# Recurrent scan of a decoder: products on single 32x32 diagonal blocks in place of block-diagonal 128x128 matrices

## The chip, the core and the metric

The kernel runs on one core of a Trainium2 chip. The metric is the device time of one execution in microseconds, as the median of several executions. The core has TensorE (matrix products, results in PSUM), VectorE (DVE), ScalarE (ACT), GpSimd (POOL) and the DMA queues, which SyncE (SP) issues. Each engine runs its own instructions in order and waits for the others on semaphores.

## The reference, cut to what matters

The whole program is a decoder of two layers (RWKV-7 time mixing, cross attention, a mixture of experts, four Mamba layers, feature attention, a quantised feed-forward part). The change touches only the recurrence of the RWKV-7 part, for 4 sequences of 512 tokens with 4 heads of 64 channels:

```python
def step(S, inp):
    rt, dt, kt, vt, at, bt = inp
    sa = jnp.einsum('bhij,bhj->bhi', S, at)
    S = S * dt[:, :, None, :] + sa[..., None] * bt[:, :, None, :] + vt[..., None] * kt[:, :, None, :]
    y = jnp.einsum('bhij,bhj->bhi', S, rt)
    return (S, y)
_, ys = jax.lax.scan(step, S0, (r_, decay, k_, v_, a_, b_))
```

## The kernel before, in words

`rwkv_scan` (from L658) does this recurrence in chunks of 32 tokens. One turn of its loop treats a tile of 128 tokens, that is 4 chunks (NCH) for each of 4 heads (H1), and there are 16 turns (NT); the first and the last are written out, the others are a hardware loop on every engine. A turn consists of these steps, in TensorE's order:

1. `tr` (L955): six 128x128 transposes bring the decayed keys of the tile to token rows; ACT copies them to `tm`.
2. `levels` (L945): for each head, 32 small products (64 rows by 32 columns of weights) give four 32x32 matrices per chunk: BA, BR, KA, KR. DVE picks the causal entries level by level into `Ac` (L875). Between heads, `state_step` (L928) carries the state of the previous tile through one chunk, and DVE adds it up (L854). `state_y` (L936) multiplies the states by `RT`; ACT copies the outputs (L769).
3. POOL spreads the four compact matrices of each head to block-diagonal 128x128 matrices `Abd` (L750): it multiplies a broadcast copy by a mask of blocks.
4. `q` (L970, L971): for each head a transpose of BA, and KA times the values. ACT copies both into `PQX` (L781, L782).
5. The doubling, called the k steps below (L981 to L983): (1 - A)^-1 times the right-hand side X = [W | U] by five steps X += P X, with P and its transpose Q squared each time. Steps run k = 0 to 4, and heads h = 0 to 3 within each. A head's step has a product for Q (L981), one for P (L982), both left out at k = 4, and one for X (L983), all 128x128x128 on block-diagonal matrices. ACT copies P and Q out of PSUM (L786), DVE adds X (L883). After k = 0 DVE's queue has `decay(it + 1)` for the next turn (L816 to L821), and after k = 1 ACT's queue has `factors(it + 1)` (L762, L763).
6. `rp` (L987): W times BR; DVE adds it into `RT` (L888) and then makes the factors of the next turn (L832 to L846).
7. `mn` (L995 to L997): 48 products of 32 rows by 64 columns give the transfer matrices of the chunks. DVE writes `MT` (L897) and ACT `NN` (L791); the next turn's `tr` waits for both.
8. `y1`: two products with zeros clear two banks (L1003), then BR times U and KR times the values are added (L1005, L1006). POOL copies the next values to `vs` after it (L744).

A wait is written in two ways. `wait_ge` alone leaves the wait to the instruction that follows. `hold` (L71 to L75) waits with an instruction of its own, which also adds 1 to a semaphore `passed`; in the trace it is an EVENT_SEMAPHORE of line L75, with an ALU_OP or FUSED_REGOPS of L74 for the value waited for. Each fp32 product of TensorE stands as two records of LDWEIGHTS and MATMUL in the trace, so 12 products are 24 records.

Of the kernel before, what the change touches and what calls it, by code (L numbers as in the profile page):

```python
# [165 lines left out]
def shape_constants():  # L166
# [3 lines left out]
    for w in (32, 16, 8):  # L170
# [13 lines left out]
        "block_mask": np.repeat((np.arange(P)[:, None] // 32 == np.arange(4)[None]).astype(np.float32)[:, :, None], 32, 2),  # L184
# [473 lines left out]
def rwkv_scan(nc, g, m):  # L658
# [15 lines left out]
    with ExitStack() as ctx:  # L674
# [11 lines left out]
        Abd = [sb(f"rs_Abd{h}", [P, 4, P]) for h in range(H1)]  # L686
        PQX = [sb(f"rs_PQX{h}", [P, 3 * P]) for h in range(H1)]
# [4 lines left out]
        blockmask = sb("rs_blockmask", [P, NCH, CH])  # L692
# [6 lines left out]
        BA, BR, KA, KR = range(4)  # L699
# [9 lines left out]
        pool = signal("pool", "vs " + each("xa") + each("bd"))  # L709
# [21 lines left out]
        with nc.Block() as block:  # L731
            @block.sync
            def _(sp):
                for dst, src in ((levelmask, g["level_masks"]), (blockmask, g["block_mask"]), (reset, g["chunk_reset"]),
                                 (eye64, g["eye_twice"]), (bound, g["carry_bound"])):
                    sp.dma_start(full(dst), src).then_inc(masks_in, 16)

            @block.gpsimd
            def _(po):
                begin(po, pool)  # L740
                po.wait_ge(masks_in, 80)
                with po.Fori(0, NT) as it:
# [3 lines left out]
                    for h in heads:  # L746
                        nc.gpsimd.tensor_copy(PQX[h][:, 2 * P:2 * P + N1], tm[:, AT, h * N1:(h + 1) * N1]).then_inc(*pool(f"xa{h}"))  # L747
                    for h in heads:
                        po.wait_ge(*dve.at(f"ac{h}{LAST}", it))
                        nc.gpsimd.tensor_tensor(  # L750
                            Abd[h][:, :, :].rearrange("p m (q t) -> p m q t", q=NCH),
                            Ac[h][:, :, :, :].rearrange("p x y (o t) -> p (x y) o t", o=1).broadcast_to([P, 4, NCH, CH]),
                            blockmask[:, :, :].rearrange("p (o q) t -> p o q t", o=1).broadcast_to([P, 4, NCH, CH]),
                            ALU.mult).then_inc(*pool(f"bd{h}"))

            @block.scalar
            def _(a):
# [14 lines left out]
                def body(it, state=True, following=True):  # L772
# [6 lines left out]
                    for h in heads:  # L779
                        a.wait_ge(*pe.at(f"q{h}", it))  # L780
                        nc.scalar.activation(PQX[h][:, P:2 * P], bank[h][:, P:2 * P], ACT.Copy)  # L781
                        nc.scalar.activation(PQX[h][:, 2 * P + N1:], bank[4 + h][:, N1:P], ACT.Copy).then_inc(*act(f"q{h}"))  # L782
                    for k in range(4):
                        for h in heads:
                            a.wait_ge(*pe.at(f"n{h}{k}", it))
# [2260 lines left out]
```

## Time and profile before

| | us |
|---|---|
| median of 3 runs | 3923.72 (3921.09 to 3923.76) |
| the profiled execution | 3921.58 |
| its span in the trace | 3919.7 |
| busy: TensorE, DVE, ACT, POOL | 3082.4, 2929.5, 1879.3, 1883.7 |
| the scan's part of the span | about 228 to 847 |

The profile's page gives busy times and costly groups of instructions by line. Answers of the trace then show one stretch of time, one engine or one line. In a timeline, a row is one or several like instructions in a row: start, time from the first start to the last end, engine, line, operation, output and inputs, shape, count, and in brackets the idle time before with what ended it. PEclk is the share of full TensorE clock that was granted: 0.50 is the lower of its two levels (1.2 GHz), 1.00 the higher (2.4 GHz).

### The profile page before, as it was taken

What the parts mean: (1) busy time and instruction counts of PE and PEld (TensorE: products, weight loads), DVE (VectorE), ACT (ScalarE), POOL (GpSimd) and SP (SyncE); (2) the same over time, 40 slices, a digit from 0 to 9 for tenths busy, and PEclk for the clock granted to TensorE, in tenths of its full rate; (3) what the DMA queues carried; (4) which work ended last, traced back from release to release, by engine and by line L of the source; (5) the groups of instructions that cost most, each with busy time, mean ns of one, the idle gap of its engine ahead of it and who ended that gap; (6) DMA issues with size and microseconds to landing.
All of it is one profiled execution on the core that took longest, in us unless ns stands there. A gap on an engine that the chain in (4) does not pass through costs nothing. (4 is left out here: it accounts for less than half of the span.)

```text
span 3919.7 us, 46678 instructions
## 1 busy us (share of the span) xinstructions
PE 3082.4 (79%) x16262; PEld 1734.7 (44%) x16262; DVE 2929.5 (75%) x3862; ACT 1879.3 (48%) x2899; POOL 1883.7 (48%) x961
## 2 busy tenths in 40 slices
PE   8968888865638965898889988899888998666823
PEld 3457777753325742333434334343343443333512
DVE  4656666665711123999999999999999999996588
ACT  2433333222411114766677666677666775523434
POOL 0011111121221021779888888888888888861100
PEclk9967777777858986999999999999999999997966
DMA  1000000000032323344443444434444444331000
GB/s 42 0 7 1 0 0 0 0 6 19 0 109 87 117 79 102 129 149 140 162 140 133 148 141 161 143 130 158 141 152 143 135 153 140 129 118 35 1 20 22
DMA packets 120614, 342.23 MB, mean 87 GB/s; under 512 B 14763, under 2 KB 45698, under 8 KB 119714
## 3 DMA queue, kind: packets, MB, share of 16 engines
q1 hardware_dynamic: 114594, 332.01, 25.0%
q0 software_dynamic: 3072, 6.00, 0.8%
q10 hardware_dynamic: 2816, 2.62, 0.2%
q8 instruction: 64, 1.05, 0.1%
q14 instruction: 68, 0.56, 0.0%
HBM read 328.31 MB, written 14.68 MB: 88 GB/s over the span
## 5 line engine op out<-in xcount | busy, mean ns | idle before, releaser
L1950 POOL TENSOR_TENSOR mb_h<-mb_h,mb_BC 128x1024 f32<-128x1024 f32 x512 | 1212.8, 2389 | 406.8 <-DVE mb_h L2197 406.8
L2197 DVE TENSOR_TENSOR_SCAN mb_h<-mb_dA,mb_bx 128x1024 f32<-128x1024 f32 x512 | 1170.5, 2286 | 23.8 <-ACT mb_dA L2064 6.0
L2300 PE MATMUL mb_y<-mb_h,ident 128*128 128x512 f32 x2048 | 1000.0, 628 | 215.2 <-POOL mb_h L1950 213.4
L2064 ACT ACTIVATE mb_dA<-mb_delta,mb_A 128x511 f32<-128x511 f32 x1024 | 664.7, 713 | 415.3 <-DVE mb_h L2197 409.4
L2300 PEld LDWEIGHTS mb_y<-mb_h,ident 128*128 128x128 f32 x2048 | 387.7, 198 | 790.2 <-issue 415.3
L2193 DVE TENSOR_TENSOR mb_bx<-mb_du,mb_BC 128x1024 f32<-128x1024 f32 x512 | 630.3, 1231 | 42.7 <-DMA mb_BC<-mamba_BC 6.7
L744 POOL COPY rs_vs<-rw_v 128x256 f32 x16 | 9.8, 612 | 571.2 <-PE rs_p L1006 338.9
L245 PE MATMUL mb_p<-mb_xT,mb_in_w 128*128 128x512 f32 x512 | 238.1, 609 | 23.3 <-ACT mb_sz L1990 16.7
L245 PE MATMUL mb_p<-mb_upad,mb_convd 128*128 128x512 f32 x512 | 225.0, 592 | 0.8 <-ACT mb_upad L1978 0.8
L1674 DVE TENSOR_TENSOR me_h<-me_s,me_p 128x320 f32<-128x320 f32 x64 | 31.2, 488 | 242.6 <-ACT me_s L1651 242.6
L883 DVE TENSOR_TENSOR rs_PQX<-rs_p,rs_PQX 128x128 f32<-128x128 f32 x320 | 85.8, 290 | 114.8 <-PE rs_p L983 113.7
L245 PEld LDWEIGHTS mb_p<-mb_xT,mb_in_w 128*128 128x128 f32 x512 | 99.1, 196 | 153.5 <-issue 118.9
L1628 POOL DMA_INDIRECT me_y<-expert_results,slot x32 | 30.8, 963 | 256.2 <-DMA expert_results<-me_oe 246.8
L245 PEld LDWEIGHTS mb_p<-mb_upad,mb_convd 128*128 128x128 f32 x512 | 96.8, 189 | 124.1 <-issue 124.1
L245 PE MATMUL me_p<-me_xeT,me_W 128*128 128x320 f32 x512 | 141.4, 437 | 0.9 <-ACT me_xeT L1639 0.9
L786 ACT ACTIVATE rs_PQX<-rs_p 128x256 f32<-128x256 f32 x256 | 93.1, 383 | 71.6 <-PE rs_p L983 71.6
L245 PE MATMUL mb_p<-mb_out_w,mb_yg 128*128 128x256 f32 x512 | 121.0, 379 | 0.0
L2064 ACT ACT_TABLE_LOAD x91 | 116.8, 1283 | 1.6
L245 PEld LDWEIGHTS me_p<-me_xeT,me_W 128*128 128x128 f32 x512 | 97.5, 192 | 43.7 <-issue 4.8
L750 POOL TENSOR_TENSOR rs_Abd<-rs_Ac,rs_blockmask 128x512 f32<-128x512 f32 x64 | 81.0, 1266 | 65.8 <-DVE rs_Ac L875 65.5
L2389 POOL TENSOR_TENSOR fa_A<-fa_E,fa_sm 128x512 f32<-128x512 f32 x32 | 35.8, 1122 | 149.0 <-DVE fa_sm L2516 144.3
L875 DVE COPY_PREDICATED rs_Ac<-rs_levelmask,rs_p 128x64 f32<-128x64 uint32 (+1 forms) x256 | 62.8, 246 | 54.1 <-POOL rs_PQX L747 17.0
(439 smaller groups left out, 5554.2 us busy)
## 6 DMA issues: line engine op xcount, KB each, us to landing
mb_BC<-mamba_BC SPq DMA_DIRECT2D x256, 1024.0 KB, 5.2
me_W<-in_L_ffn_W SPq DMA_DIRECT2D x24, 1024.0 KB, 9.2
mb_in_w<-in_L_attn_in_proj_w SPq DMA_DIRECT2D x4, 1024.0 KB, 8.2
mb_convd<-in_mamba_taps SPq DMA_DIRECT2D x4, 1024.0 KB, 10.2
expert_rows<-me_zero SPq DMA_DIRECT2D x1, 2560.0 KB, 10.1
x<-in_x SPq DMA_DIRECT2D x4, 512.0 KB, 5.3
me_xe<-expert_rows SPq DMA_DIRECT2D x8, 256.0 KB, 10.7
expert_results<-me_oe ACTq DMA_DIRECT2D x8, 256.0 KB, 7.6
```

The source lines that it names most:

```text
L245: i = nc.tensor.matmul(out, lhsT, rhs, start=k == 0, stop=k == len(pairs) - 1)
L750: nc.gpsimd.tensor_tensor(Abd[h][:, :, :].rearrange("p m (q t) -> p m q t", q=NCH), Ac[h][:, :, :, :].rearrange("p x y (o t) -> p (x y) o ...
L786: nc.scalar.activation(PQX[h][:, 0:2 * P], bank[h][:, 0:2 * P], ACT.Copy).then_inc(*act(f"n{h}{k}"))
L875: nc.vector.copy_predicated(later(Ac[h][:, :, :, :].rearrange("p x y t -> p (x y) t"), l), later(levelmask[:, l, :].rearrange("p (k t) -> ...
L883: nc.vector.tensor_tensor(X, bank[4 + h][:, 0:P], X, ALU.add).then_inc(*dve(f"x{h}{k}"))
L1674: nc.vector.tensor_tensor(h[:, k, :], s1[:, k % 2, :], bank[3 + 2 * (k % 2)][:, 0:CAP], ALU.mult).then_inc(*dve(f"h{k}"))
L1950: tt(hk, hk, buffer(k, it)[:, 1, :, :], ALU.mult).then_inc(*pos(f"hc{k}{part}"))
L2064: i = av(dA[k % 2][:, c, s, 1:], delta[:, it % 2, mc, 1:], ACT.Exp, scale=A[:, MC * layer(it) + mc, n:n + 1])
L2193: tt(full(bx), du[c][:, :].rearrange("p (o t) -> p o t", o=1).broadcast_to([P, SU, T]), buffer(k, it)[:, 0, :, :], ALU.mult).then_inc(*dvs ...
L2197: nc.vector.tensor_tensor_scan(flat(h[k % NBUF][:, c, :, :]), flat(dA[k % 2][:, c, :, :]), flat(full(bx)), 0.0, ALU.mult, ALU.add).then_in ...
L2300: i = mm(ybank[c][:, :], m.ident[:, :], h[k % NBUF][:, c, s, :], start=False, stop=e == HALF - 1 and s == SU - 1)
L2389: nc.gpsimd.tensor_tensor(A[:, u % NE, :, :], E[:, u % NE, :, :], sm[:, u % NE, :].rearrange("p (h o) -> p h o", o=1).broadcast_to([P, HC, ...
```

## The change

The block-diagonal matrices `Abd` are gone, and with them POOL's spreading, the mask `block_mask` and its load. Every product on such a matrix becomes four products ("quads"), each on one chunk's 32x32 block, at the same partitions 32q to 32q + 31 for its weights, its moving operand and its output. P and Q shrink to 32 columns (`PQ`), so ACT copies 64 elements per partition in place of 256; X stays 128 wide. The step k = 3 leaves out Q, which k = 4 doesn't use. The transpose of BA becomes a product with the identity block. The four quads of one product write into one PSUM bank at different partitions, except in `rp`, where each goes to a bank of its own (4 to 7); DVE's addition of `RT` becomes four. TensorE's waits in `q` and in the k steps become `hold`s. DVE has one `hold` per head less, since it needn't wait for POOL before it writes `Ac`.

```diff
         Ac = [sb(f"rs_Ac{h}", [P, 2, 2, CH]) for h in range(H1)]
-        Abd = [sb(f"rs_Abd{h}", [P, 4, P]) for h in range(H1)]
-        PQX = [sb(f"rs_PQX{h}", [P, 3 * P]) for h in range(H1)]
+        PQ = [sb(f"rs_PQ{h}", [P, 2, CH]) for h in range(H1)]
+        X = [sb(f"rs_X{h}", [P, 2, N1]) for h in range(H1)]
...
-                    for h in heads:
-                        po.wait_ge(*dve.at(f"ac{h}{LAST}", it))
-                        nc.gpsimd.tensor_tensor(
-                            Abd[h][:, :, :].rearrange("p m (q t) -> p m q t", q=NCH),
...
-                            ALU.mult).then_inc(*pool(f"bd{h}"))
...
-                        nc.scalar.activation(PQX[h][:, P:2 * P], bank[h][:, P:2 * P], ACT.Copy)
-                        nc.scalar.activation(PQX[h][:, 2 * P + N1:], bank[4 + h][:, N1:P], ACT.Copy).then_inc(*act(f"q{h}"))
+                        nc.scalar.activation(PQ[h][:, 1, :], bank[h][:, CH:2 * CH], ACT.Copy)
+                        nc.scalar.activation(X[h][:, 1, :], bank[4 + h][:, N1:P], ACT.Copy).then_inc(*act(f"q{h}"))
...
                             if l == 0:
                                 hold(v, m, pe.at(f"lv{h}", it))
-                                hold(v, m, pool.at(f"bd{h}", it - 1))
...
-                    nc.vector.tensor_tensor(RT[:, :, :], bank[4][:, 0:W2].rearrange("p (c n) -> p c n", c=DC), rt_of(it), ALU.add).then_inc(*dve("rp"))
+                    for q in range(NCH):
+                        s = slice(CH * q, CH * q + CH)
+                        i = nc.vector.tensor_tensor(RT[:, :, s], bank[4 + q][:, 0:DC * CH].rearrange("p (c n) -> p c n", c=DC), rt_of(it)[:, :, s], ALU.add)
+                    i.then_inc(*dve("rp"))
...
                     for h in heads:
-                        t.wait_ge(*pool.at(f"bd{h}", it))
-                        nc.tensor.transpose(bank[h][:, P:2 * P], Abd[h][:, BA, :], m.ident[:, :])
-                        mm(bank[4 + h][:, N1:P], Abd[h][:, KA, :], vs[:, h * N1:(h + 1) * N1], start=True, stop=True).then_inc(*pe(f"q{h}"))
+                        hold(t, m, dve.at(f"ac{h}{LAST}", it))
+                        for s in quads:
+                            mm(bank[h][s, CH:2 * CH], chunks(h, BA)[s, :], m.ident[s, s], start=True, stop=True)
+                        for s in quads:
+                            i = mm(bank[4 + h][s, N1:P], chunks(h, KA)[s, :], vs[s, h * N1:(h + 1) * N1], start=True, stop=True)
+                        i.then_inc(*pe(f"q{h}"))
                     for k in range(5):
                         for h in heads:
                             if k == 0:
-                                t.wait_ge(*act.at(f"q{h}", it))
+                                hold(t, m, act.at(f"q{h}", it))
+                                if h == 0:
+                                    hold(t, m, pool.at(f"xa{H1 - 1}", it))
                             else:
-                                t.wait_ge(*act.at(f"n{h}{k - 1}", it))
-                                t.wait_ge(*dve.at(f"x{h}{k - 1}", it))
-                            Pk = PQX[h][:, 0:P] if k else Abd[h][:, BA, :]
+                                hold(t, m, act.at(f"n{h}{k - 1}", it))
+                                hold(t, m, dve.at(f"x{h}{k - 1}", it))
+                            Pk, Qk = (PQ[h][:, 0, :] if k else chunks(h, BA)), PQ[h][:, 1, :]
+                            if k < 3:
+                                for s in quads:
+                                    mm(bank[h][s, CH:2 * CH], Pk[s, :], Qk[s, :], start=True, stop=True)
                             if k < 4:
-                                mm(bank[h][:, P:2 * P], Pk, PQX[h][:, P:2 * P], start=True, stop=True)
-                                mm(bank[h][:, 0:P], PQX[h][:, P:2 * P], Pk, start=True, stop=True)
-                            mm(bank[4 + h][:, 0:P], Pk, PQX[h][:, 2 * P:3 * P], start=True, stop=True).then_inc(*pe(f"n{h}{k}"))
+                                for s in quads:
+                                    mm(bank[h][s, 0:CH], Qk[s, :], Pk[s, :], start=True, stop=True)
+                            for s in quads:
+                                i = mm(bank[4 + h][s, 0:P], Pk[s, :], X[h][s, :, :].rearrange("p x i -> p (x i)"), start=True, stop=True)
+                            i.then_inc(*pe(f"n{h}{k}"))
...
-                        i = mm(bank[4][po:po + N1, hp * P:(hp + 1) * P], W[h], Abd[h][:, BR, :], start=True, stop=True)
+                        for q, s in enumerate(quads):
+                            i = mm(bank[4 + q][po:po + N1, hp * CH:hp * CH + CH], W[h][s, :], chunks(h, BR)[s, :], start=True, stop=True)
...
-                        mm(y_out(h), Abd[h][:, BR, :], U[h], start=False, stop=False)
-                        i = mm(y_out(h), Abd[h][:, KR, :], vs[:, h * N1:(h + 1) * N1], start=False, stop=False)
+                        for s in quads:
+                            mm(y_out(h)[s, :], chunks(h, BR)[s, :], U[h][s, :], start=False, stop=False)
+                        for s in quads:
+                            i = mm(y_out(h)[s, :], chunks(h, KR)[s, :], vs[s, h * N1:(h + 1) * N1], start=False, stop=False)
```

## Rows read from the trace of the kernel before

**Rows 1.** The page's head.
```profile
span 3919.7 us, 46678 instructions
```

**Rows 2.** Windows: stretch, length, busy us (instructions) per engine, granted clock; one turn.
```profile
548.20:556.70 8.50, 7.67 (x318) 6.36 (x316) 5.18 (x21) 0.75 (x3) 4.04 (x7) 0.50 0.00 0
556.70:560.40 3.70, 2.79 (x15) 2.80 (x16) 2.05 (x4) 1.91 (x10) 1.79 (x2) 0.50 0.00 0
560.40:571.20 10.80, 10.03 (x83) 9.78 (x83) 6.22 (x20) 7.23 (x16) 0.00 (x0) 0.95 0.00 0
...
574.90:577.80 2.90, 2.90 (x96) 2.85 (x95) 2.77 (x4) 0.00 (x0) 0.00 (x0) 1.00 0.00 0
577.80:581.80 4.00, 3.89 (x22) 3.68 (x20) 4.00 (x10) 0.00 (x0) 0.00 (x0) 0.60 0.00 0
```

**Rows 3.** Timeline of DVE in the same turn.
```profile
550.12 1.43 DVE L875 COPY_PREDICATED rs_Ac<-rs_levelmask,rs_p 128x64 f32<-128x64 uint32 x4 [0.97 <-POOL rs_PQX L747]
...
563.89 0.69 DVE L816 TENSOR_TENSOR_SCAN rs_dif<-rs_reset,rw_w 128x256 f32<-128x256 f32 x1
...
566.64 0.88 DVE L883 TENSOR_TENSOR rs_PQX<-rs_p,rs_PQX 128x128 f32<-128x128 f32 x4
...
575.03 0.42 DVE L888 TENSOR_TENSOR rs_RT<-rs_p,rs_rt 128x256 f32<-128x256 f32 x1 [0.93 <-PE rs_p L987]
...
581.32 1.62 DVE L897 SCALAR_TENSOR_TENSOR rs_MT<-rs_eye,rs_Eend,rs_p 128x64 f32<-128x64 f32 x8
```

**Rows 4.** Timeline of ACT in the same turn.
```profile
556.64 0.45 ACT L769 ACTIVATE rw_w<-rs_p 128x128 f32 x2 [7.75 <-PE rs_p L936]
...
566.75 1.49 ACT L762 ACTIVATE rs_Ep<-rs_dif 128x1536 f32<-128x1536 f32 x1
...
569.30 1.19 ACT L786 ACTIVATE rs_PQX<-rs_p 128x256 f32<-128x256 f32 x4
```

**Rows 5.** Timeline of TensorE's matrix products in the same turn.
```profile
552.81 1.29 PE L945 MATMUL rs_p<-rs_left,rs_right 64*32 64x32 f32 x64
...
555.51 0.36 PE L936 MATMUL rs_p<-rs_S,rs_RT 64*32 64x64 f32 x4
555.59 0.33 PE L945 MATMUL rs_p<-rs_left,rs_right 64*32 64x64 f32 x4
...
557.61 0.47 PE L970 MATMUL rs_p<-ident,rs_Abd 128*128 128x128 f32 x1 [1.11 <-POOL rs_Abd L750]
...
558.19 0.42 PE L970 MATMUL rs_p<-ident,rs_Abd 128*128 128x128 f32 x1
...
562.24 0.39 PE L982 MATMUL rs_p<-rs_Abd,rs_PQX 128*128 128x128 f32 x2
...
566.97 0.49 PE L981 MATMUL rs_p<-rs_PQX 128*128 128x128 f32 x2 [0.77 <-DVE rs_PQX L883]
...
574.15 0.66 PE L987 MATMUL rs_p<-rs_Abd,rs_PQX 128*64 128x128 f32 x8 [0.39 <-DVE rs_PQX L883]
...
577.82 0.71 PE L1003 MATMUL rs_p<-ident,rs_zeros 128*128 128x128 f32 x4
...
583.90 1.52 PE L955 MATMUL rs_p<-ident,rs_base 128*128 128x128 f32 x6 [2.20 <-ACT rs_NN L791]
```

**Rows 6.** Lines L945 (552.79 to 553.49) and L74 (553.4 to 553.6): counts, first and last start.
```profile
L945 PE MATMUL rs_p<-rs_left,rs_right x52: 237/238/291, 552.8 to 553.5; 64*32 64x32 f32 x48, 64*32 64x64 f32 x4
...
L74 PEldq ALU_OP  x1: 32/32/32, 553.5 to 553.5; - x1
```

**Rows 7.** Line L75, the holds: TensorE's 557.0 to 557.45, DVE's 549.7 to 550.1.
```profile
L75 PEldq EVENT_SEMAPHORE  x2: 51/51/51, 557.1 to 557.4; - x2
...
L75 DVEq EVENT_SEMAPHORE  x2: 21/21/21, 549.8 to 550.0; - x2
```

**Rows 8.** Timelines of DVE in the last turn and of SyncE before the scan.
```profile
839.54 1.62 DVE L897 SCALAR_TENSOR_TENSOR rs_MT<-rs_eye,rs_Eend,rs_p 128x64 f32<-128x64 f32 x8 [2.65 <-PE rs_p L997]
...
228.53 0.43 SPq L736 DMA_DIRECT2D rs_blockmask<-in_block_mask  x1
```

More of the change, by code:

```diff
@@ L698, in rwkv_scan @@
         AT, BT, KT = range(3)
-        BA, BR, KA, KR = range(4)
+        BA, BR, KA, KR = ((x, y) for x in range(2) for y in range(2))
         heads = range(H1)
@@ L708, in rwkv_scan @@
         act = signal("scalar", "tm " + each("q") + " ".join(f"n{h}{k}" for k in range(4) for h in heads) + " nn")
-        pool = signal("pool", "vs " + each("xa") + each("bd"))
+        pool = signal("pool", "vs " + each("xa"))
         dvf, acf = signal("vector_f", "cum dif left right base end"), signal("scalar_f", "ep em")
@@ L733, in _ @@
             def _(sp):
-                for dst, src in ((levelmask, g["level_masks"]), (blockmask, g["block_mask"]), (reset, g["chunk_reset"]),
+                for dst, src in ((levelmask, g["level_masks"]), (reset, g["chunk_reset"]),
                                  (eye64, g["eye_twice"]), (bound, g["carry_bound"])):
@@ L740, in _ @@
                 begin(po, pool)
-                po.wait_ge(masks_in, 80)
+                po.wait_ge(masks_in, 64)
                 with po.Fori(0, NT) as it:
@@ L780, in body @@
                         a.wait_ge(*pe.at(f"q{h}", it))
-                        nc.scalar.activation(PQX[h][:, P:2 * P], bank[h][:, P:2 * P], ACT.Copy)
-                        nc.scalar.activation(PQX[h][:, 2 * P + N1:], bank[4 + h][:, N1:P], ACT.Copy).then_inc(*act(f"q{h}"))
+                        nc.scalar.activation(PQ[h][:, 1, :], bank[h][:, CH:2 * CH], ACT.Copy)
+                        nc.scalar.activation(X[h][:, 1, :], bank[4 + h][:, N1:P], ACT.Copy).then_inc(*act(f"q{h}"))
                     for k in range(4):
                         for h in heads:
+                            n = 2 if k < 3 else 1
                             a.wait_ge(*pe.at(f"n{h}{k}", it))
-                            nc.scalar.activation(PQX[h][:, 0:2 * P], bank[h][:, 0:2 * P], ACT.Copy).then_inc(*act(f"n{h}{k}"))
+                            nc.scalar.activation(PQ[h][:, 0:n, :], bank[h][:, 0:n * CH].rearrange("p (x t) -> p x t", x=n), ACT.Copy).then_inc(*act(f"n{h}{k}"))
                         if following and k == 1:
@@ L881, in body @@
                             v.wait_ge(*pe.at(f"n{h}{k}", it))
-                            X = PQX[h][:, 2 * P:3 * P]
-                            nc.vector.tensor_tensor(X, bank[4 + h][:, 0:P], X, ALU.add).then_inc(*dve(f"x{h}{k}"))
+                            nc.vector.tensor_tensor(X[h][:, :, :], bank[4 + h][:, 0:P].rearrange("p (x i) -> p x i", x=2), X[h][:, :, :], ALU.add).then_inc(*dve(f"x{h}{k}"))
                         if following and k == 0:
@@ L916, in _, with chunks @@
                 begin(t, pe, pes)
-                W = [PQX[h][:, 2 * P:2 * P + N1] for h in heads]
-                U = [PQX[h][:, 2 * P + N1:3 * P] for h in heads]
+                W = [X[h][:, 0, :] for h in heads]
+                U = [X[h][:, 1, :] for h in heads]
+                quads = [slice(CH * q, CH * q + CH) for q in range(NCH)]
+                def chunks(h, kind):
+                    return Ac[h][:, kind[0], kind[1], :]
                 half = [(h // 2, N1 * (h % 2)) for h in heads]
```

8 lines of the change are left out of this document (2 added, 6 removed).

## The prediction

> **What bounds the kernel now.** I read the page first (a span of 3919.7 us [rows 1], the profiled execution 3921.58). The change lies in the recurrent scan alone, from about 228 to 847 us, in 16 turns, so at most a sixth of the time can move. Next come the windows over one turn. TensorE is busy nearly throughout: 7.67 of 8.50 us in the levels, 10.03 of 10.80 in the k steps, all 2.90 of `mn` [rows 2]. That makes it a suspect, but who ends the turn is read from the timelines. `rp` starts at 574.15 [rows 5], DVE adds it at 575.03 and works on without a gap up to `MT`, 581.32 plus 1.62 [rows 3]. After ACT's NN copies TensorE starts the next `tr` at 583.90, idle 2.20 us before it [rows 5]. So from `rp` on DVE sets the turn; `mn`, whose successor L1003 starts at 577.82 [rows 5], `y1` and their price on TensorE are hidden beside it. From `tr` to `rp` it is a chain through TensorE, with two stretches that others set: DVE's `decay` after k = 0 (from 563.89 up to the first x of k = 1 at 566.64 [rows 3], TensorE idle 0.77 before 566.97 [rows 5]), and ACT's factors after k = 1 (from 566.75, next copy of P and Q at 569.30 [rows 4]).
>
> The granted clock is the third thing to see. It is 0.50 in the levels and in `q`, 0.95 over the k steps of full matrices, 1.00 in `mn`, and 0.60 on average over the 4 us behind `mn` [rows 2].
>
> **Price of one small product.** The levels are the nearest rows: 64 records in 1.29 us, each about 0.31 at the end [rows 5], so their starts lie within 0.98, at the low clock. They stream 48 x 32 + 16 x 64 = 2560 columns (the two forms in part: [rows 6]). On four column tiles at once that is 640 columns a tile in about 0.98 + 0.09, or 1.67 ns a column. At the high clock a pair of 128-column records takes 0.39 with a tail of 0.28 [rows 5], 0.11 a record or 0.87 ns a column. A head's k step (k < 3) now streams 2 x (32 + 32 + 128) = 384 columns in each of four tiles: 0.64 us at the low clock, 0.33 at the high. Before it is six records of 0.11, 0.67. So at the low clock the small blocks gain next to nothing per step; a quarter of the columns, and half the clock, and X is still 128 wide.
>
> **Which clock.** The levels, 90% busy with 64x32 tiles, never raise it; after `mn`, 2.90 us without a gap on 32x64 tiles, it falls [rows 2]. Both say that small tiles don't hold it. What raises it before is the full 128x128 work of `q` and k = 0. I take the low clock for the whole scan. The first part of k = 0 was at the low clock already: it ran from 559.8 (557.61 + 0.58 + 3 x 0.53 for `q`, below) to its last x, which ends at `decay`'s start, 563.89 [rows 3]: 4.05 with 0.5 of tail, so 3.55 us, and there the blocks gain 1 us.
>
> **Holds on TensorE.** After ACT's end at 557.09 [rows 4] come two holds [rows 7] and the first product at 557.61 [rows 5]: 0.51 us for a pair, some 0.24 each. Each k step now has such a pair ahead of its products. The queue covers it in part: when TensorE's sequencer got to the next L74 at 553.5, 52 of the 64 records had started, so 12 ran behind [rows 6]. In a k step the last 12 of 24 records are eight of X and four of P, (2 x 128 + 32) x 1.67 = 0.48 us: about the price of the pair, 0.44 without the landing of the wait. So it is hidden for k < 3, nearly for k = 3 (0.53 us of work), and shows at k = 4, where a head's eight records are 0.43: I take 0.50. Bounds: nothing (all hidden), and 0.24 for each of 20 steps, near 5 us a turn, if the queue doesn't run ahead over such a wait. The rows are nearer the first.
>
> **One turn, step by step.**
> - Levels: DVE has one hold fewer per head. Its two stand at 549.8 and 550.0 [rows 7], 0.2 us, with the first copy at 550.12 [rows 3]. The chain DVE, state_step, levels passes it on once to TensorE: -0.2.
> - Start of `q`: it follows two holds behind ACT's copy, not POOL, whatever the row's releaser says (POOL's first matrix is done long before). The third hold adds 0.1 beyond what overlaps: 557.61 becomes 557.5. POOL's 81 us of spreading were beside this chain, so their removal is worth nothing by itself.
> - `q`: 0.58 us a head (557.61 to 558.19 [rows 5]; later ones 0.53), because a record has 128 weight columns. New: 2 x (32 + 64) x 1.67 = 0.32. Four heads 1.28, k = 0 starts at 558.8 in place of 559.8.
> - k = 0: 4 x 0.64, ends 561.35. Last x 0.6 later, 561.95 (before 563.85).
> - k = 1: hidden under `decay`, which takes 2.75 [rows 3]. First x of k = 1 at 565.0, k = 2 starts at 565.1 (before 566.97).
> - k = 2: 2.56, to 567.7. ACT's factors start behind `decay`, 2.6 us: 567.4, next copy 567.6, so k = 3 at 567.75.
> - k = 3: 4 x 0.53, to 569.9. k = 4: 3 x 0.50 + 0.43 and a tail of 0.2, to 572.05. Last x 572.35. `rp` at 572.4, before 574.15: -1.75.
> - `rp` itself: 32 records of 32 columns on up to eight tiles, 0.3 to 0.5 with its tail against 0.66 [rows 5], -0.2; DVE's four additions against one of 0.42, +0.35 (from 0.2 each).
> - From here DVE goes as before, so the turn ends 1.6 us earlier. What is late next: `mn` at the low clock needs 96 x 64 columns on two tiles, 5.1 us from 572.8, 577.9, against DVE's being ready for `MT` at 579.7, so a cover of 1.8. `y1` then takes 0.85 for the zeros and 64 records of 64 columns on four tiles, 1.7, to 580.6, against `tr` at 582.3. `vs` is wanted only in the next `q`.
>
> Outside the turns: one load of five on SP less, 0.43 us [rows 8], -0.5. In the last turn nothing lies between `RT` and `MT` (DVE idle 2.65 there [rows 8]), so `mn`'s 2.2 us more show and eat that turn's gain: +0.5. Sum: 15 x -1.6 = -24, nothing for the last two. 3921.6 - 24 = 3897.6. The median of the runs is 2 us above the profiled execution, so I say 3899.
>
> **Rivals.**
> 1. The clock rises in the k steps, or the steps are cheaper than 1.67 ns a column says. A head then costs 0.52 at least by the pair of holds (0.44 plus 12 records of 0.08), or 0.33 if that is hidden too. `decay` and the factors then set the middle: a gain of 2 to 4.4 us a turn, 3890 to 3855. For it: nothing in the rows but the busy time. Chance 0.17, at 3885.
> 2. The holds and the issue of 24 records aren't hidden. At 0.1 us more for each of the 16 steps that aren't under `decay`, the gain is gone: 3921, chance 0.12; with 0.24 unhidden it is +2.2 us a turn, 3957, chance 0.05.
> 3. Slower: the four quads of a product don't run at once, because they are row tiles that write one PSUM bank. In the levels the four tiles at once share their rows; where two sets of rows run interleaved, `state_y` in between the levels [rows 5], they write different banks. So no row shows what this change needs. In turn, a step costs 4 x 0.64 = 2.56: k = 0, 2, 3, 4 together add some 25 us a turn and k = 1 another 6; with `q` and `y1`, about 34, or 4460. Two at a time gives +10 a turn, 4080. It decides from a factor of 1.2 over 0.64 on (8.96 us of steps outside `decay` times 0.2 are the gain of 1.75). Chance 0.13, at 4080 to 4460.
> 4. It doesn't do what it says: the k steps shrink but `mn` or `y1` at the low clock becomes the end of the turn by running over its cover of 1.8. It needs 3.4 us over the forecast 5.1 to eat the 1.6 of gain too; then about 3923 and more, chance 0.03.
>
> The Trainium skill bears on the third. "TensorEngine Tiling (Array Packing)", Restrictions and Gotchas, says that different row tiles cannot access the same PSUM bank simultaneously. By that the time would be the 4460 above. "PSUM — Partial Sum Buffer", PSUM bank collisions, allows different quadrants of one bank at once, and by it the sum stands. No row here tells them apart.
>
> **How the numbers follow.** Forecast 3899, chance 0.50, its own range 3885 to 3913 (0.9 us a turn either way). Something above 0.2% (8 us) can be told from no change. Faster: 0.50 + 0.17 and a little of the second rival, 0.70; within 0.2%: 0.12; slower: 0.18. For 8 in 10 the range leaves out the third rival and the worst of the first and second: 3864 to 3927.
>
> **What would show it.** Right: in the windows PEclk 0.50 from the levels to `y1`; a head's k step 0.64 apart and k = 4 0.50; L883's first x of k = 1 right behind `decay`; `mn` near 5.1 us with no DVE wait before `MT`; turns 1.6 us shorter. Wrong: starts of four quads that lie a whole record apart (third rival); idle time of TensorE in front of each head's products with L75 in it (second); PEclk 1.00 in k = 1 to 4 (first); DVE idle in front of L897 in the middle turns (fourth).

## The result, and the profile after

The changed kernel takes 3980.88 us (median of 4 runs, 3976.19 to 3988.15), the kernel before 3922.40 beside it (4 runs, 3917.29 to 3923.76). The ratio is 1.0153, 95% interval 1.0134 to 1.0173: slower by 58 us, where I had forecast 23 us faster and a range that ended at 3927.

First the head of the page after, and its line of the DMA queue that fetches instructions (packets, MB, share of 16 engines).

```profile
span 3981.7 us, 60064 instructions
...
q8 instruction: 210, 3.44, 0.4%
```

And the same queue's line on the page before.

```profile
q8 instruction: 64, 1.05, 0.1%
```

There are 13,386 more instructions than in [rows 1], and 146 more instruction loads of 16 KB. The same queue over one middle turn of the changed kernel (577 to 619 us):

```profile
q8 instruction: 9, 0.15, 1.5%
```

Over a turn of before (548 to 586 us) the same view has no packet at all. So TensorE's hardware loop, which before ran without fetching, now loads its whole body again in every turn. (That loop has 15 turns on TensorE: there only turn 0 is written out, and the last turn is in the loop.) By the trace's records TensorE has 1197 instructions in a turn before and 2047 after; a small product is two records of LDWEIGHTS and two of MATMUL whatever its size, and four quads are sixteen.

The branch that closes this loop is the plainest line (L1010 before, L1021 after; the columns are count, shortest, median and longest in ns, first and last start). The kernel before:

```profile
L1010 PEldq FUSED_REGOPS  x15: 53/59/59, 276.2 to 803.9; - x15
...
L1010 PEldq COMPARE_BRANCH  x15: 76/208/242, 314.6 to 839.9; - x15
```

The changed kernel:

```profile
L1021 PEldq FUSED_REGOPS  x15: 53/59/63, 287.0 to 867.3; - x15
...
L1021 PEldq COMPARE_BRANCH  x15: 83/3532/3817, 327.1 to 904.3; - x15
```

The median branch takes 3532 ns in place of 208; the shortest of each row, 76 and 83, is the loop's exit. The FUSED_REGOPS stands once at the head of each turn, so its first and last start give the mean turn: (803.9 - 276.2) / 14 = 37.69 us before, (867.3 - 287.0) / 14 = 41.45 after, +3.76. Fourteen of these are 52.6 us, nearly all of the result. I use this mean for every kernel below; where there is no loop, it is worked out in the same way from the starts of `tr`.

Windows of one turn, to be held against [rows 2] (stretch, length, busy us and instructions of TensorE, weight loads, DVE, ACT and POOL, granted clock, DMA share, GB/s); the stretches are levels, `q`, k steps, `rp`, `mn`, and the rest:

```profile
578.40:589.33 10.93, 8.75 (x321) 7.14 (x321) 6.06 (x25) 1.32 (x4) 0.77 (x4) 0.50 0.01 3
589.33:590.67 1.34, 1.34 (x65) 1.30 (x66) 0.20 (x1) 0.72 (x6) 0.00 (x0) 0.50 0.05 12
590.67:607.00 16.33, 12.50 (x392) 7.51 (x384) 8.24 (x27) 6.39 (x22) 0.00 (x0) 0.81 0.01 3
607.00:608.00 1.00, 0.99 (x40) 0.99 (x42) 0.04 (x1) 0.00 (x0) 0.00 (x0) 0.50 0.07 16
608.00:612.60 4.60, 4.60 (x94) 4.60 (x90) 4.52 (x8) 0.00 (x0) 0.00 (x0) 0.50 0.01 4
612.60:618.53 5.93, 3.22 (x70) 2.63 (x69) 3.63 (x14) 0.79 (x4) 0.40 (x1) 0.50 0.01 3
```

And TensorE's timeline of the same turn, in answer to [rows 5]:

```profile
577.01 1.51 PE L953 MATMUL rs_p<-ident,rs_base 128*128 128x128 f32 x6 [3.58 <-ACT rs_NN L783]
...
587.06 0.32 PE L943 MATMUL rs_p<-rs_left,rs_right 64*32 64x64 f32 x2 [0.39 <-issue]
...
590.88 0.61 PE L990 MATMUL rs_p<-rs_X,rs_Ac 32*32 32x128 f32 x3
592.48 0.64 PE L990 MATMUL rs_p<-rs_X,rs_Ac 32*32 32x128 f32 x4 [1.00 <-issue]
...
594.63 0.32 PE L985 MATMUL rs_p<-rs_PQ 32*32 32x32 f32 x4
...
595.27 0.32 PE L985 MATMUL rs_p<-rs_PQ 32*32 32x32 f32 x4
...
596.38 0.41 PE L990 MATMUL rs_p<-rs_X,rs_PQ 32*32 32x128 f32 x4 [0.26 <-issue]
...
598.59 0.23 PE L985 MATMUL rs_p<-rs_PQ 32*32 32x32 f32 x5 [0.65 <-DVE rs_X L873]
...
599.14 0.23 PE L985 MATMUL rs_p<-rs_PQ 32*32 32x32 f32 x5
...
600.66 0.41 PE L990 MATMUL rs_p<-rs_X,rs_PQ 32*32 32x128 f32 x6 [0.41 <-issue]
...
607.01 0.68 PE L996 MATMUL rs_p<-rs_Ac,rs_X 32*64 32x32 f32 x32 [0.41 <-DVE rs_X L873]
```

The rows with "issue" are in the middle of a group of like products, between which nothing is waited for: L990 stops after three or four of its eight records at 590.9 and goes on at 592.48. These are the seams between loaded blocks. (The rows of L985 are heads of k = 1 and k = 2; they are used further down.) The end of the turn shows on DVE [rows 3] and ACT [rows 4]:

```profile
607.96 0.61 DVE L880 TENSOR_TENSOR rs_RT<-rs_p,rs_rt 128x64 f32<-128x64 f32 x4 [1.01 <-PE rs_p L996]
...
614.62 1.61 DVE L890 SCALAR_TENSOR_TENSOR rs_MT<-rs_eye,rs_Eend,rs_p 128x64 f32<-128x64 f32 x8
```

```profile
616.26 0.79 ACT L783 ACTIVATE rs_NN<-rs_p 128x128 f32<-128x128 f32 x4 [12.15 <-DVE rs_MT L890]
```

ACT's last NN copy ends at 617.05, but TensorE's sequencer is in the branch until 618.5, and the next `tr` starts at about 618.9 (its first recorded product stands at 619.25, with two of the six missing). Before, `tr` followed 0.14 us behind ACT (582.97 + 0.79 against 583.90 in [rows 5]). So of a branch of 3.4 us some 1.7 are on the path; the rest lies beside DVE and ACT.

By stages, this turn against the one of before: `tr` to `q` 12.3 against 11.2; `q` 1.34 against 2.14; k steps 16.3 against 14.4; `rp` to the next `tr` 11.9 against 9.75. That is +1.1, -0.8, +1.9, +2.1. Turn 0, which stands as straight code ahead of the loop, went the other way: its `tr` and the next stand at 245.18 and 281.08 before, 257.04 and 289.96 after, 35.90 against 32.92. Both versions load there, four blocks before and seven after.

The profiled executions differ by another 12 us ahead of the scan, where no instruction of this change stands: TensorE's clock there is 0.87 before and 0.77 after between 80 and 120 us. In the other profiles the scan begins at 245.0 (pad_220) to 257.5 us (flat_after). Whether the change has a part in that, one profile of each kernel can't tell. The explanation is of the scan's own part, 52 us.

### The profile page after: what moved, and what is told of

It reads as the page before. It is cut to its first block and busy times, and to the rows that moved or that the text cites. A ratio compares the mean times of both kernels' runs of the same rounds, so it can differ in the third digit from the quotient of the medians.

```text
span 3981.7 us, 60064 instructions
## 1 busy us (share of the span) xinstructions
PE 3093.9 (78%) x22726; PEld 1663.5 (42%) x22726; DVE 2923.1 (73%) x3910; ACT 1833.2 (46%) x2899; POOL 1798.5 (45%) x897
## 5 line engine op out<-in xcount | busy, mean ns | idle before, releaser
L873 DVE TENSOR_TENSOR rs_X<-rs_p,rs_X 128x128 f32<-128x128 f32 x320 | 89.1, 289 | 145.1 <-PE rs_p L990 142.9
L990 PE MATMUL rs_p<-rs_X,rs_PQ 32*32 32x128 f32 x2048 | 145.7, 333 | 22.6 <-issue 20.5
L778 ACT ACTIVATE rs_PQ<-rs_p 128x64 f32<-128x64 f32 (+1 forms) x256 | 53.4, 216 | 120.6 <-PE rs_p L990 119.9
```

Source lines behind the costliest of these rows:

```text
L778: nc.scalar.activation(PQ[h][:, 0:n, :], bank[h][:, 0:n * CH].rearrange("p (x t) -> p x t", x=n), ACT.Copy).then_inc(*act(f"n{h}{k}"))
L873: nc.vector.tensor_tensor(X[h][:, :, :], bank[4 + h][:, 0:P].rearrange("p (x i) -> p x i", x=2), X[h][:, :, :], ALU.add).then_inc(*dve(f"x ...
L990: i = mm(bank[4 + h][s, 0:P], Pk[s, :], X[h][s, :, :].rearrange("p x i -> p (x i)"), start=True, stop=True)
```

## The experiments

The names: `pad` kernels are the kernel before with idle products added, `flat` ones have TensorE's turns written out in place of its hardware loop, `boxes`, `fit`, `nest` and `nest3` are variants of the changed kernel.

| kernel | us (runs) | ratio to before, 95% | mean turn | TensorE records of code / executed per turn | loads per turn | branch, median ns |
|---|---|---|---|---|---|---|
| before | 3922.4 (4) | | 37.69 | 1197 / 1197 | 0 | 208 |
| after | 3980.88 (4) | 1.0153 [1.0134, 1.0173] | 41.45 | 2047 / 2047 | 9.9 | 3532 |
| pad_100 | 3939.19 (1) | | 38.63 | 1597 / 1597 | 0 | 208 |
| pad_125 | 3981.37 (1) | | 41.39 | 1697 / 1697 | 4.5 | 229 |
| pad_220 | 4088.47 (1) | | 49.15 | 2077 / 2077 | 9.9 | 4412 |
| boxes | 3973.65 (2) | 1.0132 [1.0096, 1.0167] | 40.64 | 1905 / 1905 | 9.0 | 3346 |
| flat_after | 3932.55 (1) | | 37.72 | straight / 1991 | 7.8 | none |
| flat_before | 3926.80 (1) | | 37.67 | straight / 1158 | 4.5 | none |
| fit | 3910.15 (6) | 0.9959 [0.9945, 0.9973] | 36.96 | 1747 / 1747 | 9.0 | 3633 |
| fit_twowaits | 3967.11 (2) | 1.0101 [1.0078, 1.0125] | 40.33 | 1791 / 1791 | 9.0 | 3407 |
| nest | 3875.31 (4) | 0.9874 [0.9855, 0.9893] | 35.01 | 1552 / 1752 | 0 | 209 |
| nest_twowaits | 3926.80 (8) | 1.0003 [0.9991, 1.0015] | 37.81 | 1588 / 1796 | 5.1 | 3297 |
| nest3 | 3889.53 (4) | 0.9907 [0.9881, 0.9933] | 35.49 | 1418 / 1818 | 0 | 209 |
| nest3_twowaits | 3927.24 (10) | 1.0003 [0.9991, 1.0016] | 37.71 | 1446 / 1862 | 0 | 209 |

Loads are the queue's packets between two starts of `tr`, averaged over the middle turns. For the kernels with an inner loop the code is the executed count less the repeats of a pass (four heads of 48 records and two per wait).

### Does a longer loop body alone do it? pad_100, pad_220, and later pad_125

```diff
                     i.then_inc(*pe("y1"))
+                    if state:
+                        for k in range(220):
+                            s = slice(CH * (k % 4), CH * (k % 4) + CH)
+                            mm(bank[6][s, 511:512], zeros[0:CH, 0:CH], m.ident[0:CH, 0:1], start=True, stop=True)
```

> The kernel before with 100 one-column products more at the end of each turn of TensorE's loop, where TensorE waits for the next turn; the loop body grows from 1197 to about 1597 recorded instructions. Fetch theory (the loop of the changed kernel lost its time because its body no longer stays in TensorE's instruction memory and is loaded again in each turn): the body still stays, no 16 KB instruction loads in the middle turns, turns of 37.5 to 38.5 us, about 3922 to 3935 us. Rivals (the added waits on TensorE, the lower clock): they say nothing of padding, the same 37.5 to 38.5 us.

> The kernel before with 220 such products more in each turn, about 2077 recorded instructions, as long a body as that of the changed kernel (2047), but with the block-diagonal products, waits and clock of before. Fetch theory: about nine 16 KB loads a turn, stalls inside groups of products, turns 3 to 8 us longer than with 100 products, 3970 us or more. Rivals (waits, clock): only the products themselves, at most 2.5 us a turn more than with 100, under 3965 us, and no loads.

The branch of pad_100, then that of pad_220:

```profile
L1014 PEldq COMPARE_BRANCH  x15: 76/208/242, 325.9 to 861.0; - x15
```

```profile
L1014 PEldq COMPARE_BRANCH  x15: 79/4412/4816, 325.4 to 1008.2; - x15
```

TensorE's timeline of pad_220 at the end of a turn, through its idle products and into the next `tr`:

```profile
611.84 0.94 PE L1011 MATMUL rs_p<-ident,rs_zeros 32*32 32x1 f32 x83
614.63 1.88 PE L1011 MATMUL rs_p<-ident,rs_zeros 32*32 32x1 f32 x128 [1.85 <-issue]
618.10 1.12 PE L1011 MATMUL rs_p<-ident,rs_zeros 32*32 32x1 f32 x67 [1.59 <-issue]
624.48 0.88 PE L955 MATMUL rs_p<-ident,rs_base 128*128 128x128 f32 x3 [5.26 <-issue]
```

A hundred idle products cost 0.94 us a turn and bring no load (65 packets on the whole page, against 64). Another 120 cost 10.5 us a turn, with nearly ten loads. The products themselves explain little of it: their records follow within 1.88 us for 128, so 120 products, 240 of these records, are 3.5 us at most. The rest is in the seams, 1.85 and 1.59 within a row of products that wait for nothing, and 5.26 at the jump back. The kernel before with nothing but a longer loop is 166 us slower. That is more than I had expected: 10.5 us a turn over pad_100 in place of 3 to 8; pad_100 itself lies just above its range of 37.5 to 38.5.

The row of 128 is worth a second look. With as many records of LDWEIGHTS it is 256 records, and it stands between two seams, so it is what one block of 16 KB holds. It runs off in 1.88 us, and the next row starts 3.47 us behind its start (614.63, 618.10). Other turns have the same row of 128, with 3.5 to 4.0 us to the next. So in this stretch a new block comes only every 3.5 to 4 us, and code that issues 256 records faster than that stands still. It also says where the 10.5 us lie: nearly all between ACT's last NN copy and the next `tr` (10.84 us against 0.42 in pad_100, means of 14 turns), while the stages before agree within 0.2 us, although blocks are loaded in them too. So 10.5 us is the price behind very short products, not that of every body of this length.

pad_125 looked for the edge.

> The kernel before with 125 padding products, about 1697 instructions, between 1597 (stays, 38.2 us a turn) and 1747 (loaded again). Fetch theory with eight blocks of 256 of which one is used to load ahead: 1697 needs seven or eight blocks by where it starts; if it stays, 38.4 us a turn; if not, nine loads and more than 42 us a turn.

```profile
L1014 PEldq COMPARE_BRANCH  x15: 76/229/4836, 326.8 to 902.2; - x15
```

Twenty-five products more than pad_100 give +2.8 us a turn. It is neither of the two outcomes that I had named: turns with three loads alternate with turns with six, and branches of some 0.22 us with branches of 4.6 to 4.8. So the body ceases to stay somewhere between 1597 and 1697 records here. It isn't the count of records alone: nest_twowaits, with some 1588 records of code, still loads three to nine blocks a turn. What else decides, such as where the body starts within a block, was not varied.

### Is it the loop, or the loads as such? flat_after, flat_before

```diff
-                with t.Fori(1, NT) as it:
+                for it in range(1, NT):
                     body(it)
```

> The changed kernel with TensorE's 16 turns written out one after another, no hardware loop on TensorE (the other engines keep theirs). Fetch theory: every instruction is still loaded, nine loads a turn and the stalls of 0.7 to 1.6 us inside groups of products stay, but the 3 us at the jump back go: turns of 37 to 39 us, 3915 to 3945 us. Waits theory: waits against constants need no register work, 0.09 us of some 0.24 less a wait, 42 waits: 37 to 38 us too, but with no gap inside groups of products. Clock theory: 41 us as before.

> The kernel before with TensorE's turns written out one after another, so every instruction is loaded once. 1197 instructions a turn or fewer, about five loads a turn. Fetch theory: stalls where 256 instructions run off faster than a load comes in, in the levels above all; 0 to 2 us a turn more, 3920 to 3950 us. Waits and clock theories: faster than before by the register work, 37 us a turn, 3910 us.

Written out, the changed kernel's turn falls to 37.72 us (from 41.29, when that one too is counted by the starts of `tr`), although it still loads 7.8 blocks a turn (62 packets in 300 us). The kernel before written out loads 4.5 a turn and its turn stays at 37.67.

The time alone doesn't settle it, since written-out code changes the waits too: a wait for a constant has no ALU_OP of L74 in front (1991 records a turn in place of 2047), and the theory of the waits had forecast 37 to 38 us as well, but with no gap inside a group of products. The waits are cheaper indeed. At k = 4 the heads of flat_after, with two waits each, are 0.30 us apart in the median over 14 turns, those of the changed kernel 0.49. One such stretch on flat_after's DVE, the last head of k = 3 and three of k = 4, 0.29 apart:

```profile
463.19 1.15 DVE L873 TENSOR_TENSOR rs_X<-rs_p,rs_X 128x128 f32<-128x128 f32 x4 [0.19 <-PE rs_p L990]
```

But the gaps inside groups are there, in one turn of 37.1 us (us in total, times, longest):

```profile
PE rs_p L990 <- issue: 4.6, 3, 2.0
```

And the gain doesn't lie in the k steps, where most of the waits are: from the first x to the last they take 13.6 us in the loop and 13.9 written out (means of 14 turns, as all here). It lies from `tr` to the first x (16.0 to 13.3) and between ACT's last NN copy and the next `tr` (1.44 to 0.15), that is, at the jump back and in the blocks that come after it. So most of the 3.6 us goes with a loop whose body doesn't stay; how much of it is the cheaper waits, no run tells. A load isn't free where the code runs straight on, as the gaps show, but it can be hidden there, as in flat_before. Why a loop's blocks after the jump come later than straight ones, no run here tells either.

### Which part of the change? boxes

The block-diagonal matrices of BR and KR come back, with POOL's spreading for them, so that `rp` and `y1` are one product each in place of four; `q` and the k steps stay as changed.

```diff
-                        for q, s in enumerate(quads):
-                            i = mm(bank[4 + q][po:po + N1, hp * CH:hp * CH + CH], W[h][s, :], chunks(h, BR)[s, :], start=True, stop=True)
+                        i = mm(bank[4][po:po + N1, hp * P:(hp + 1) * P], W[h], Abd[h][:, 0, :], start=True, stop=True)
...
-                        for s in quads:
-                            mm(y_out(h)[s, :], chunks(h, BR)[s, :], U[h][s, :], start=False, stop=False)
+                        mm(y_out(h), Abd[h][:, 0, :], U[h], start=False, stop=False)
```

> The changed kernel with rp and y1 on block-diagonal matrices again (POOL spreads BR and KR alone); k steps and q on small blocks. TensorE's body has 144 x 2 recorded instructions fewer in these parts less one wait, about 1905. Fetch theory: if this fits, the turn falls to 33 to 36 us, 3840 to 3890 us, without loads; if it still doesn't (the limit is not known better than between 1197 and 2047), 38 to 41 us with about eight loads a turn. Waits theory: the k steps are as in the changed kernel, so 40 us a turn and about 3965 us. Clock theory: likewise.

0.8 us a turn come back, and the loop still loads nine blocks. Removing 142 records isn't enough to make the body stay, so this says little of `rp` and `y1`.

### The waits: fit and fit_twowaits

`fit` goes on from boxes: KA is block-diagonal too, DVE transposes BA (32x32 blocks), and ACT's copy and DVE's addition of a head count up one semaphore, so that a head's products in k = 1 to 4 wait once. fit_twowaits is the same with two.

```diff
-                                hold(t, m, act.at(f"n{h}{k - 1}", it))
-                                hold(t, m, dve.at(f"x{h}{k - 1}", it))
+                                hold(t, m, (both[h], it * 8 + 2 * k))
```

> A shorter TensorE body with the small blocks kept in the k steps: P, Q and X on single blocks; rp, y1 and KA times the values on block-diagonal matrices again (POOL); the transpose of BA by DVE on 32x32 blocks in place of TensorE; one wait in place of two before each k step (ACT's copy and DVE's addition of a head raise one semaphore). About 1761 recorded instructions. Fetch theory: a body of at most 1793 stays whatever block boundary it starts at, if eight blocks of 256 are held; no loads in the middle turns, turns of 33.5 to 36 us, 3845 to 3890 us. If loads go on, eight or nine a turn, the limit is lower and turns are 37 to 39 us. Waits theory: half the waits give back half the loss, 39 us a turn, 3945 us. Clock theory: granted clock stays at 0.5 to 0.6 in the k steps, turn as in the changed kernel, 41 us.

> The same with two waits before each k step as in the changed kernel; about 1793 recorded instructions. Price of the waits alone: 16 steps with 0.24 us more on TensorE's queue, hidden in part; fetch theory: 0 to 2 us a turn over the one with one wait, up to 30 us in all, if it still has no loads; if it has them, 5 us a turn over it. Waits theory: 4 us a turn over it without loads.

Both load nine blocks a turn and both have branches of 3.4 to 3.6 us, and yet fit is faster than before by 0.4%. The second wait costs 3.4 us a turn. With loads in both it can't be told how much of this is the wait's own; the next pairs take the loads away.

### Shorter code for the same work: nest and nest_twowaits

k = 1 and 2 have the same products, so they become an inner hardware loop on TensorE.

```diff
-                    for k in range(5):
...
+                    with t.Fori(1, 3) as k:
+                        for h in heads:
+                            step(h, 1, both_done(h, k))
+                    pe.next += H1
+                    for k in (3, 4):
+                        for h in heads:
+                            step(h, k, both_done(h, k))
```

> The kernel with one wait (fit) and TensorE's k steps 1 and 2, which are the same instructions, as an inner hardware loop of two rounds: the same work and the same order, but some 200 instructions fewer in the body, about 1550, under the 1597 that still stayed with padding (fit has 1747 and is loaded again, nine loads a turn). Fetch theory: no loads in the middle turns, 3 to 5 us a turn less than fit (36.5), 32 to 34 us, 3835 to 3875 us. Waits or clock theory: as fit, 3910 us, or a little more for the inner loop's jump.

> The same with two waits before each k step, as the changed kernel has them, about 1580 instructions, so without loads: the price of the second wait by itself. By the trace a wait takes 0.24 us of TensorE's sequencer; in fit against fit_twowaits it went with 3.5 us a turn, both with loads. If that was the wait's own price: 3.5 us a turn over nest again (56 us in all). If it was mostly loads that come later: 0 to 2 us a turn (0 to 30 us).

nest executes 1752 records a turn, more than fit's 1747, and computes the same; only its code is 200 records shorter. Its page and its branch:

```profile
q8 instruction: 66, 1.08, 0.1%
```

```profile
L1037 PEldq COMPARE_BRANCH  x15: 67/209/209, 310.0 to 795.8; - x15
```

Two microseconds a turn gone (36.96 to 35.01), 35 us in all, and a kernel 1.3% faster than before. This is the cleanest price of the loading, nine blocks a turn with the same work and the same waits, and it is less than the 3 to 5 us that I had expected. nest_twowaits was to give the price of the second wait alone, but its somewhat longer code began to load again (branch 67/3297/4343), so its 2.8 us a turn are of both causes.

### The second wait without loads: nest3 and nest3_twowaits

k = 3 goes into the inner loop too, at the price of a Q that nobody reads.

```diff
-                    with t.Fori(1, 3) as k:
+                    with t.Fori(1, 4) as k:
```

> As nest (small blocks in the doubling, the rest block-diagonal, one wait per k step), but the inner hardware loop holds k = 1, 2 and 3, so that TensorE's code for a turn is shorter again by about a twelfth, some 1500 records in place of 1560. For that k = 3 computes a Q that nobody reads, four products of 32 columns a head, which costs 0.11 us a head at the low clock and 0.06 at the high one, at most 0.43 us a turn. Both theories: no instruction loads in the turns, a turn of 34.8 to 35.3 us, and 3875 to 3883 us. It is the partner of the next run. Should it be clearly faster than nest (under 3870), a shorter loop body gains beyond the absence of loads, which neither theory expects.

> As nest3, but with the changed kernel's two waits of their own ahead of each head's products in k = 1 to 4, in place of one. With nest the second wait made 51 us, but instruction loads came back with it, 5 a turn, so it isn't known which of the two cost what. Here the code for a turn stays under the length at which loads began. Theory 1 (a wait of its own costs 0.24 us on TensorE's sequencer, and at the high clock a head's products, 0.22 to 0.35 us, don't cover a pair of 0.5): no loads, and up to 16 times 0.2 us less what decay and the factors hide anyway, 2 to 3 us a turn over nest3, 30 to 50 us in all, 3908 to 3930. Theory 2 (the queue hides the second wait, as the prediction had it, and nest's 51 us came from the loads): no loads, at most 0.5 us a turn over nest3, 3875 to 3888.

Neither loads (65 packets on both pages, branch 209). nest3 lies 0.5 us a turn over nest, the unread Q, and above the 3883 that I had expected as its end. The k steps of a turn, first in nest3, then in nest3_twowaits:

```profile
435.75:448.00 12.25, 9.77 (x417) 8.30 (x416) 8.04 (x27) 5.89 (x19) 0.00 (x0) 0.79 0.00 0
```

```profile
445.10:459.30 14.20, 10.88 (x417) 6.58 (x416) 8.26 (x27) 5.90 (x19) 0.00 (x0) 0.92 0.00 0
```

The same 417 records of products, 1.95 us longer, at a higher granted clock; the other stages agree within 0.2 us. DVE's additions in nest3 show the pace of k = 2 and of k = 3 and 4 (twelve in two rows):

```profile
442.82 1.33 DVE L891 TENSOR_TENSOR rs_X<-rs_p,rs_X 128x128 f32<-128x128 f32 x4 [0.23 <-PE rs_p L995]
445.48 2.38 DVE L891 TENSOR_TENSOR rs_X<-rs_p,rs_X 128x128 f32<-128x128 f32 x8 [1.34 <-PE rs_p L995]
```

In nest3_twowaits each stands in a row of its own, with DVE waiting in front; k = 3, then k = 4:

```profile
454.88 0.29 DVE L890 TENSOR_TENSOR rs_X<-rs_p,rs_X 128x128 f32<-128x128 f32 x1 [0.79 <-PE rs_p L994]
455.50 0.29 DVE L890 TENSOR_TENSOR rs_X<-rs_p,rs_X 128x128 f32<-128x128 f32 x1 [0.33 <-PE rs_p L994]
...
457.39 0.29 DVE L890 TENSOR_TENSOR rs_X<-rs_p,rs_X 128x128 f32<-128x128 f32 x1 [0.37 <-PE rs_p L994]
457.91 0.29 DVE L890 TENSOR_TENSOR rs_X<-rs_p,rs_X 128x128 f32<-128x128 f32 x1 [0.23 <-PE rs_p L994]
```

With one wait the heads are 0.35 apart (1.33 - 0.29 over three steps), the pace of the products at the high clock; with two they are 0.62 apart, and 0.50 at k = 4, the pace of the waits. The second wait costs 2.2 us a turn (37.71 - 35.49), 38 us in all: within what the first theory gave (30 to 50), and far over the second's 0.5. nest3_twowaits, with the small blocks in the doubling, a loop that stays and two waits, takes as long as the kernel before.

## Why the prediction was wrong

**The term that was missing.** The sum counted the products and the waits of a turn and took for granted that TensorE's instructions are there when their turn comes. The change takes a turn from 1197 to 2047 records, and pad_220 shows that a body of that length is loaded again in every turn of this loop, and costs time, with nothing else changed. I had read the page for its span and had not looked at the queue q8, whose 64 packets with none in a turn say that the loop stays. No rival had it either; the slower rival was another mechanism (four quads in turn), and it fell. For the changed kernel itself flat_after gains 3.6 us a turn, most of it at the jump back and behind it, though its waits are cheaper too. The nearest pair that differs in the inner loop alone, fit_twowaits against nest3_twowaits, gives 2.6 us for nine loads a turn (40.33 - 37.71), and that although nest3_twowaits computes the unread Q. With one wait it is 1.95 (fit against nest).

The Trainium skill has the mechanism: "Runtime: NRT & Kernel Launch", Instruction fetch mechanics, gives TensorE an instruction memory of 128 KiB or 2048 instructions, refilled in blocks of 16 KiB, and says that crossing a block's edge is "mostly hidden". The packets of 16 KB and the 256 records between two seams of pad_220 agree. The runs bear out "mostly hidden" for flat_before, and not for pad_220 and flat_after, with seams of 1.2 to 2.0 us. The rule that prefetch hides the loads would have left my 3899 as it was. The same section warns that a taken branch out of a window of two blocks stalls until its target is fetched. The jumps back of 3.3 to 4.8 us in the loops that load are of that kind; but loops of 1552 and 1597 records, more than six blocks of 256, jump back in 0.21 us without a load, so the window isn't two blocks for TensorE here. Nor did the loops stay up to the 2048: one of 1697 records was loaded again, and with an inner loop one of 1588 already.

**The step on the clock failed.** I took the low clock for the whole scan. It was 0.50 in the levels, `q`, `mn` and `y1`, as said, but 0.81 over the k steps and 0.99 between 596.4 and 606.7. That small tiles don't hold the high clock, read from `mn`, is not so in the k steps.

**The step on the holds failed with it.** I had the pair of holds hidden by twelve queued records of 0.48 us, which is their time at the low clock. At the low clock it is right: in the changed kernel the heads of k = 1 come 0.64 apart with two waits each (594.63, 595.27 above), which is the products' own time. At the high one the same records take half as long, and the pair shows: 0.55 to 0.70 a head in the changed kernel's k = 2 (598.59, 599.14; the median over 14 turns is 0.70, seams included) and 0.62 in nest3_twowaits. The first rival had it, 0.52 at least by the pair of holds. Its mistake was to call this a gain of 2 us a turn or more; in nest3_twowaits the k steps take 14.2 us against 14.4 before, a gain of 0.2. The second rival, that the holds aren't hidden, came true too, but at the high clock only. At k = 4 the forecast of 0.50 held.

**Both together, without loads.** The stages of nest3_twowaits (levels 11.3, k steps 14.2) with the changed kernel's `q` (1.34) and its `rp` to `MT` (0.37 longer than before) give about 37.0 us against 37.5 before. That is an estimate, since the change as it is, in a loop that stays, wasn't tried. So of my 1.6 us a turn some 0.5 would have been left even so; of the gap to the measured turn (1.6 + 3.8 = 5.4) about 1.1 is the clock and the holds, and the rest, 4.3, is put down to instruction loading. The pair above shows 2.6 of it directly, at a shorter body (1791 records).

**What held.**
- The price of a column. At 0.50 the heads of k = 0 start 0.64 apart (three rows of nest3's TensorE):

```profile
435.79 0.33 PE L990 MATMUL rs_p<-rs_PQ,rs_Ac 32*32 32x32 f32 x8
...
436.43 0.33 PE L990 MATMUL rs_p<-rs_PQ,rs_Ac 32*32 32x32 f32 x8
...
437.07 0.33 PE L990 MATMUL rs_p<-rs_PQ,rs_Ac 32*32 32x32 f32 x8
```

- So the third rival fell: four quads on different partitions of one bank run at once. 384 columns in 0.64 us is 1.67 ns a column, the price in the levels, and not four times it. Of the two pages of the Trainium skill, "TensorEngine Tiling (Array Packing)", Restrictions and Gotchas, doesn't agree with this trace. The Trainium skill's "PSUM — Partial Sum Buffer", PSUM bank collisions, agrees in its rule by quadrants, which it gives for two different engines; for two writes of TensorE it quotes the same restriction on row tiles, and that part doesn't agree.
- `q`: 1.28 us for four heads forecast, 1.34 measured.
- DVE's four additions to `RT` cost 0.37 (607.96 to 614.62 is 6.66; [rows 3] have 6.29 from 575.03 to 581.32), forecast 0.35. `rp`'s own gain of 0.2 isn't seen: its records start at 607.01 and DVE at 607.96, 0.95 against 0.88 before.
- `mn` at the low clock takes 5.1 us (607.5 to 612.6), as forecast, and `MT` at 614.62 has no idle time in front, so the fourth rival fell.
- Levels: the hold fewer on DVE was to give 0.2. nest3, which has it too (its DVE waits for POOL), can't tell; the changed kernel's levels are longer by the loads. It stays open.
- Turn 0, straight code, gained 3.0 us, where I had 1.6. It isn't explained by the sum of a middle turn either, and one turn was all it was worth. It too has its waits against constants.
- The sums hold but for two slips that change nothing: by its own rows k = 0 took 4.1 us before, not 4.05, and the first x of k = 1 would have come at 564.7, not 565.0.

## What to carry to other kernels

Before a product is cut into pieces inside a hardware loop, count the loop's instructions on that engine, and look at the instruction queue: no packet in a turn means that the body stays, and some hundred records more can cost several microseconds a turn. Where it comes near the edge, an inner loop over equal steps shortens the code without less work (fit to nest, -35 us). And price a wait of its own against the fastest pace of the products behind which it is to hide, the high clock's, and let several producers count up one semaphore where a consumer needs them all (-38 us between the nest3 kernels, -57 between the fit ones, which load).

## What the runs showed of the hardware

- A TensorE loop of 1597 records ran without a load, one of 1697 with 4.5 loads a turn on average, one of 1747 with 9, one of 2077 with 9.9 (pad_100, pad_125, fit, pad_220). One of 1588 with an inner loop loaded 5.1 (nest_twowaits). Its branch takes 208 ns where the body stays, and 3.3 to 4.4 us at the median where it doesn't.
- A block of instructions held 256 records, and behind 32x32 products of one column the next came 3.5 to 4 us later, though they ran off in 1.9 (pad_220). Nine loads a turn cost 1.95 us with the same work and waits (fit against nest).
- Straight code with 4.5 loads a turn took as long as the loop without loads (flat_before, 37.67 us against 37.69), with 39 records a turn fewer. With 7.8 loads it had gaps of 4.6 us in one turn (flat_after).
- The same pair of waits let the heads of k = 4 follow every 0.49 us in a loop and every 0.30 us in straight code, where no ALU_OP goes ahead of a wait (medians of after and flat_after).
- 32x32 products on small blocks reached the high clock for 10 us at a time (0.99 from 596.4 to 606.7), but the 32x64 products of `mn` and the levels stayed at 0.50 in the changed kernel. In nest3_twowaits `mn` ran at 1.00 (459.3 to 463.0), as it did before the change, so it isn't the shape alone.
- In a loop a second wait ahead of a head's 24 records of products costs 0.27 us a head at the high clock (0.62 - 0.35), and nothing at the low one.
